# Layer 0's 32 experts as 24 tiles of 128 hidden units, earlier loads of their combine rows, and 64-row masks in layer 1's attention

## What the kernel computes

```python
scores = sigmoid(x @ gate_w.T)
topk_ids = top_k(scores + e_bias, 4)
combine = zeros(T, E) with the normalised scores at topk_ids
g = einsum('th,ehi->tei', x, w1)
u = einsum('th,ehi->tei', x, w3)
a = silu(g) * u * combine[:, :, None]
out = einsum('tei,eih->th', a, w2)
```

## Time and profile before

| | us |
|---|---|
| median of the three timed runs | 1730.03 |
| lowest and highest of them | 1722.28, 1730.83 |
| the profiled execution | 1734.56 |
| its span, first to last instruction | 1732.8 |
| PE, DVE, ACT, POOL busy | 1441.4, 1129.3, 692.5, 170.4 |
| mean granted TensorE clock | 0.884 of full |

### The profile page before, as it was taken

One profiled execution on the slowest core, in us unless ns is written; L12 is line 12 of the kernel. 1 busy time (PEld: TensorE's weight loads), 2 busy tenths in 40 slices (PEclk: granted clock), 3 DMA queues, 4 the chain that ended last, 5 costly groups with the idle time before them and its releaser, 6 DMA issues. The chain is left out here.

```text
span 1732.8 us, 20831 instructions
## 1 busy us (share of the span) xinstructions
PE 1441.4 (83%) x6716; PEld 852.5 (49%) x6716; DVE 1129.3 (65%) x1721; ACT 692.5 (40%) x1256; POOL 170.4 (10%) x205
## 2 busy tenths in 40 slices
PE   3889999999999999429999996731699999748996
PEld 3345555554545554226666664531344444225785
DVE  4645646464646552368999998573767776146997
ACT  1133333323232333025555553421156665524663
POOL 0000100001010100001111110021011211101110
PEclk9689999999999999759999997865589998767998
DMA  2000110101010101104444441005112220112220
GB/s 72 5 9 6 25 28 7 33 0 33 0 33 0 33 4 25 28 13 105 108 108 108 108 110 38 1 1 159 36 27 57 67 57 17 30 27 84 95 91 25
DMA packets 41517, 78.47 MB, mean 45 GB/s; under 512 B 18880, under 2 KB 31048, under 8 KB 36808
## 3 DMA queue, kind: packets, MB, share of 16 engines
q1 hardware_dynamic: 40304, 69.03, 15.1%
q0 software_dynamic: 1152, 8.65, 2.4%
HBM read 69.20 MB, written 7.93 MB: 45 GB/s over the span
## 5 line engine op out<-in xcount | busy, mean ns | idle before, releaser
L582 ACT ACTIVATE shared<-ps 128x1024 f32<-128x1024 f32 (+7 forms) x256 | 165.8, 650 | 408.5 <-PE ps L428 252.1
L1216 PE MATMUL ps<-qA 128*96 128x512 f32 (+1 forms) x1152 | 305.1, 401 | 13.1 <-DVE qA L1328 10.4
L444 PE MATMUL ps<-shared,Vg 128*65 128x512 f32 (+3 forms) x768 | 295.5, 494 | 7.5 <-ACT shared L582 4.3
L495 DVE TENSOR_REDUCE mraw<-ps 128x1 f32<-128x512 f32 (+3 forms) x304 | 196.9, 660 | 112.0 <-PE ps L395 83.7
L1216 PEld LDWEIGHTS ps<-qA 128*96 128x96 f32 (+1 forms) x1152 | 192.3, 172 | 98.4 <-DVE shared L1341 21.1
L900 DVE TENSOR_REDUCE mraw<-ps 128x2 f32<-128x1024 f32 (+3 forms) x160 | 175.0, 1116 | 92.2 <-PE ps L820 68.8
L944 ACT ACTIVATE shared<-ps 128x512 f32<-128x512 f32 (+2 forms) x320 | 154.5, 562 | 138.6 <-PE ps L836 138.4
L391 PE MATMUL ps<-kH,qA 128*128 128x512 f32 (+3 forms) x384 | 185.2, 512 | 17.0 <-DVE mraw L495 13.2
L426 PE MATMUL ps<-qA,kH 128*128 128x512 f32 (+3 forms) x384 | 191.0, 498 | 2.7 <-DMA qB<-mT 2.7
L1270 ACT CAST qA<-shared 96x512 fp32r<-96x512 f32 (+1 forms) x192 | 119.2, 621 | 163.1 <-DVE shared L1348 162.5
L1227 PE MATMUL ps<-qA,kH 96*128 96x512 f32 (+1 forms) x576 | 165.4, 396 | 4.0 <-DVE qA L1322 4.0
(11 more groups left out here) (254 smaller groups left out, 1695.0 us busy)
## 6 DMA issues: line engine op xcount, KB each, us to landing
shared<-comb SPq DMA_DIRECT2D x32, 768.0 KB, 5.1
rB<-a0rec_dram POOLq DMA_DIRECT2D x8, 1024.0 KB, 7.0
shared<-comb SPq DMA_DIRECT2D x8, 1024.0 KB, 4.5
q_split<-qA SPq DMA_DIRECT2D x8, 512.0 KB
qA<-q_split SPq DMA_DIRECT2D x16, 256.0 KB, 4.4
rB<-a1rec_dram SPq DMA_DIRECT2D x32, 128.0 KB, 2.7
e0wUp<-in_w SPq DMA_DIRECT2D x64, 48.0 KB, 4.4
wqk<-in_wqk SPq DMA_DIRECT2D x8, 192.0 KB, 2.4
```

The lines of the kernel that those rows point to most:

```text
L444: ins = nc.tensor.matmul(O[0:65, lo:hi], k.Vg[par][:, kt, :], k.PT[:, slot % PTR, lo:hi], start=(kt == 0), stop=(kt == 4 * ch + 3))
L495: ins = nc.vector.tensor_reduce(out, bank[:, 0:n_h * width].rearrange("p (h w) -> p h w", w=width), AX, ALU.max)
L582: nc.scalar.activation(k.PT[:, slot % PTR, kt * P:S], score_banks(slot)[:, kt * P:S], ACT.Exp, scale=scale).then_inc(p_full, 1)
L1216: ins = nc.tensor.matmul(bank[0:M, :], w[par][:, at:at + M], h[:, cols], start=(r == 0), stop=(r == 2))
```

## The change

Three edits:

1. The 32 x 96 hidden units of layer 0, 3072 in all, are laid out on the host as 24 tiles of 128, and `stage_experts` is called with E = 24, M = 128. A tile takes units of up to two experts. 32 units never straddle an expert, so a tile has four parts of 32 partitions, each with a combine row of its own. `comb0` becomes 96 x 2048: each expert's row is stored three times, by three transfers, and each tile's rows come by four transfers, each of which broadcasts one row to 32 partitions.
2. In `stage_experts`, SP's wait ahead of the combine rows is on `f_full` (DVE's L1348 of the expert before last is done) and no longer on `a_free` (PE's down projections of it are done). This holds for both layers.
3. In layer 1's attention, each mask matmul with 128 rows becomes two with 64 rows, the identity's and the mask's upper and lower half, and `i` = 0 reads them on partitions 0 to 63, `i` = 1 on partitions 64 to 127. For that a new constant `halves` of 128 x 512 is loaded first of all and cast to bf16.

```diff
 stage_load
+        halves = k.rB[:, 0:4 * P].rearrange("p (a n) -> p a n", a=4)
         first = [
-            (cT[:, :, :], a["cT"]), (wmod[:, 0, :], a["wmod"][:, 0, :]), (k.ident[:, :], a["ident"]),
+            (halves[:, :, :], a["halves"]), (cT[:, :, :], a["cT"]), (wmod[:, 0, :], a["wmod"][:, 0, :]), (k.ident[:, :], a["ident"]),
...
                 link(nc.vector.memset(k.one_col[:, :], 1.0))
+                link(nc.vector.tensor_copy(k.halves[:, :, :, :].rearrange("p a b n -> p (a b) n"), halves[:, :, :]))
 stage_attention8, max_job
                     if diagonal:
                         for slot in range(len(js)):
-                            for i in range(2):
-                                ins = nc.tensor.matmul(pair[:, i, (slot + 1) * w - P:(slot + 1) * w], k.ident_bf[:, :],
-                                                       k.masks[:, 1, :], start=False, stop=True,
-                                                       skip_group_check=True)
+                            for part in range(2):
+                                for i in range(2):
+                                    rows = row_tile(i, 64)
+                                    ins = nc.tensor.matmul(pair[:, i, (slot + 1) * w - P:(slot + 1) * w],
+                                                           k.halves[rows, 0, part, :], k.halves[rows, 1, part, :],
+                                                           start=False, stop=(part == 1), skip_group_check=True)
 stage_combine
                 sp.wait_ge(copied, NC)
-                sp.dma_start(comb_dram, k.cT[0:E, :]).then_inc(stored, 16)
-                sp.wait_ge(stored, 16)
+                rows = comb_dram.rearrange("(e r) t -> e r t", r=copies)
+                for r in range(copies):
+                    sp.dma_start(rows[:, r, :], k.cT[0:E, :]).then_inc(stored, 16)
+                sp.wait_ge(stored, 16 * copies)
 stage_experts
-        NLD = 16 * (1 + (bias is not None))
+        parts = comb_dram.shape[0] // E
+        NLD = 16 * (parts + (bias is not None))
...
                 def load(e, par):
-                    sp.dma_start(k.cb[0:M, par, :], comb_dram[bass.ds(e, 1), :].broadcast_to((M, T)))\
-                        .then_inc(ld[par], 16)
+                    for q in range(parts):
+                        sp.dma_start(k.cb[q * M // parts:(q + 1) * M // parts, par, :],
+                                     comb_dram[bass.ds(parts * e + q, 1), :].broadcast_to((M // parts, T)))\
+                            .then_inc(ld[par], 16)
...
-                        sp.wait_ge(a_free, JOBS * (2 * j + par - 1) + 2)
+                        sp.wait_ge(f_full, JOBS * (2 * j + par - 1))
                         load(2 * j + par, par)
 program
-        stage_experts(nc, k, "e0", 32, 96, 1, k.hT, a["w1"], a["w3"], a["w2"], None, comb0, None, finish0)
+        stage_experts(nc, k, "e0", 24, P, 1, k.hT, a["w1"], a["w3"], a["w2"], None, comb0, None, finish0)
```

More of the change, by code:

```diff
@@ L1053, in stage_combine @@
         comb = sb("comb", [P, NT, E])
+        copies = comb_dram.shape[0] // E
         pick = sb("pick", [P, NT, E])
@@ L1689, in program @@
         k.masks = sb("masks", [P, 2, P], BF16)
+        k.halves = sb("halves", [P, 2, 2, P], BF16)
         k.mod = sb("mod", [P, 2, 6, B])
@@ L1718, in program @@
         dram = lambda n, s: nc.dram_tensor(n, s, F32, kind="Internal").ap()
-        comb0, comb1 = dram("comb0", (32, T)), dram("comb1", (8, T))
+        comb0, comb1 = dram("comb0", (96, T)), dram("comb1", (8, T))
         q_dram, k_dram = dram("q_split", (NH, 32, T)), dram("k_split", (NKV, 32, T))
@@ L1823, in constants @@
     pos = np.arange(S, dtype=f)
+    halves = np.zeros((P, 2, 2, P), f)
+    for part in range(2):
+        rows = slice(part * 64, (part + 1) * 64)
+        halves[:, 0, part, :] = np.tile(np.eye(P, dtype=f)[rows], (2, 1))
+        halves[:, 1, part, :] = np.tile(masks[rows, 1, :], (2, 1))
     dec = np.exp(-pos / f(S)).astype(f).reshape(TPB, P).T
@@ L1829, in constants @@
     return {
-        "ident": np.eye(P, dtype=f), "masks": masks, "dec": dec, "rope": rope,
+        "ident": np.eye(P, dtype=f), "masks": masks, "halves": halves.reshape(P, 4, P), "dec": dec, "rope": rope,
         "iota": np.tile(np.arange(32, dtype=f), (P, 1)),
@@ L1834, in constants, with packed @@
     }
+def packed(w):
+    return w.transpose(1, 0, 2).reshape(D, 24, P).transpose(1, 0, 2)
 def layout(inp):
@@ L1867, in layout @@
         "wqk0": wqk, "wo0": wo0,
-        "w1": g["L0_ffn_w1"], "w3": g["L0_ffn_w3"], "w2": g["L0_ffn_w2"],
+        "w1": packed(g["L0_ffn_w1"]), "w3": packed(g["L0_ffn_w3"]), "w2": g["L0_ffn_w2"].reshape(24, P, D),
         "W1a": W1[:, :, 0:256], "W1b": W1[:, :, 256:512],
```

## The result

The median of four runs is 1659.58 us (1651.65 to 1663.41); that of before, in four runs, is 1728.3 us (1722.28 to 1730.83). The ratio is 0.9601, with a 95% interval of 0.9556 to 0.9646: some 69 us. The profiled execution took 1658.08 us, where that of before took 1734.56; the forecast was 1664.

A forecast was written before the change was run, and what follows sets the result against it. Layer 0's experts were taken as bound by DVE's instruction chain plus GpSimd's interference. Tiles -64.3, store +2.4, first rows +0.5, constant +1.2 and masks -7 made -67.2 us, forecast 1664; 1650 to 1680 held 8 in 10.

The forecast's parts named there:

- What bounds `e0`: Layer 0's experts: DVE's chain plus GpSimd's interference sets the beat; 24 tiles at 8.75 us replace 32 experts, -64.3 us.
- PE holds the beat: Rival, layer 0's experts: the longer block vanishes in PE's backlog, 4.2 us better, 1660; chance 0.05.
- The rows' landing: Layer 0's combine rows: four pieces land after 6.3 to 6.8 us, inside 8.7 thanks to the earlier wait; cost nothing.
- rows late: Rival: combine pieces land later than 8.7 us after the wait, DVE stands each tile; 1671 to 1688; chance 0.10.
- The store and the head: Before layer 0's experts: two more stores cost +2.4 us; the first tile's rows, wanted 7.2 us after issue, +0.5.
- The constant: First stage: loading 256 KB ahead of the awaited loads costs +1.2 us; DVE's cast of it costs 0.
- The masks: Layer 1's attention: 64-row masks avoid 0.15 us per group, at most 14 us of PE, half on the path: -7 us.
- halves cost more: Rival, layer 1's attention: half masks cost more than they save, +8 in place of -7, 1679 us; chance 0.08.
- each added load costs as much as a full one: Layer 1's attention masks: 256 more weight loads each cost as much as full ones; part of the 1679 us rival, chance 0.08.
- The sum: Whole kernel: -64.3 + 2.4 + 0.5 + 1.2 - 7 = -67.2 us, forecast 1664 us.
- Its side sums: Whole kernel: forecast's own range 1650 (all the masks' gain, no longer block) to 1676, and the times given to rivals.
- slower: Rival, layer 0's experts: combine pieces don't overlap and set the beat, about 1726, or 1764 at 3.0 us each; chance 0.02.

The follow-up runs named there:

- tiles_only: Changed kernel with the masks as before and without the new constant (edits 1 and 2 alone): 1666.8 us, ratio to before 0.9627.
- no_block: Changed kernel with GpSimd's subtraction cut to 8 columns of each low part: 1646.65 us in its one run.
- split_late: Changed kernel with ACT's copies of the next tile's weights moved behind the job's SiLU instead of ahead of it: 1645.51 us, ratio to before 0.9499.
- old_wait: Changed kernel with SP's wait ahead of the combine rows back on the down projections: 1696.29 us, ratio to before 0.9787.
- masks_only: Kernel before with edit 3 alone (new constant and 64-row masks): 1729.34 us, ratio to before 0.9983.
- full_twice: Changed kernel with each half mask as a 128-row matmul, zeros in the other half's rows, same matmul count: 1677.9 us, ratio to before 0.9696.

## Why the prediction was right, step by step

- **What bounds `e0`.** Right. The beat was DVE's chain plus GpSimd's block, per instruction and not per partition. `tiles_only` and the changed kernel give 8.72 and 8.71 us per tile (8.75 forecast), the landmarks -65.2 us (-64.3 forecast), L1316 takes 0.84 us, and the long L1358 1.23 (1.26 forecast). The growth is where it was looked for: the mean of the combine product over `e0` rose from 0.842 to 0.876 us, 0.14 per tile, which is the whole step from 8.57 to 8.71 (0.175 forecast). `no_block` shows the cause: without GpSimd's work the beat falls.
- **PE holds the beat (rival).** Wrong at 8.71, since `split_late` runs the same matmuls in 8.15. But PE was nearer than the step read as: the next bound lay 0.56 us below, not at DVE's 7.92.
- **The rows' landing.** Right that they fit, and tested: 6.9 us after the first issue, just above 6.3 to 6.8, with 1.6 us to spare (1.9 forecast). The picture of pieces that follow each other at 1.22 us is what the landings show (1.2). The transfers fill 0.64 x 8.76 = 5.6 us per tile (5.7 forecast). The statement that the cover is the earlier wait stands by `old_wait`: DVE then waits in 22 of the 24 tiles and 36 us of `e0` are lost. The rival *rows late* didn't come about, but it was one wait away.
- **The store and the head.** The sizes were 2.4 and 0.5, together 2.9, and the landmark shows +2.8. They are distributed otherwise. From the store's issue to the next stage's first weights it is +2.9 (5.9 us in every run with three stores), and the head of `e0` costs nothing (-0.1). So the total is partly luck: the store's term was 0.5 too small and the head's 0.6 too large.
- **The constant.** +1.2 forecast. The first sigmoid came at 11.05, 11.16 and 11.41 us in the three kernels without it, and at 11.68 to 12.83, 12.3 on average, in the nine that load it first: +1.1. The +1.6 of the two profiles above and the +1.0 of `masks_only` (12.07) lie within that scatter. The cast is hidden, as forecast: it runs at 13.81 us, and DVE still waits for PE 4.60 us behind it.

```profile
12.66 0.21 ACT L98 ACTIVATE cT_sig<-cT 128x4 f32<-128x4 f32 x1 [10.55 <-DMA wv<-in_wv]
...
13.81 0.43 DVE L123 CAST halves<-rB 128x512 bf16<-128x512 f32 x1
...
18.84 0.25 DVE L127 COPY mod<-ps 128x12 f32<-128x12 f32 x2 [4.60 <-PE ps L105]
```

- **The masks.** -7 forecast, about -6 at an equal clock, by the step that was named: between the two row shapes PE loses time ahead of the masks and behind them, and with masks in the shape of the scores less of it. What shows it is the same stage at an equal clock with as many passes in both shapes, and the medians of the groups: 0.54 to 0.39 us in the 64 smaller ones and 0.54 to 0.33 in the 32 larger. That is some 16 us of PE (14 forecast), so a bit over a third of it was on the path and not half. `full_twice` agrees, but its 15 us hold the cost of twice the passes too; they show that the rival *halves cost more* would have held for 128-row halves. Whether PE empties its array in the step isn't shown, only the time. ACT's wait on L840 fell from 138.4 to 124.6 us, more than the forecast 7, but part of that goes with the clock: `masks_only` has 131.6. The Trainium skill, "TensorEngine Tiling (Array Packing)", section "Key Properties", says that a change of mode drains the engine; the 0.33 us ahead of `full_twice`'s masks, and 0.24 without a change, agree with it. The rival that each added load costs as much as a full one did not come about: four loads and matmuls of 64 rows took the 0.29 us of two full ones.
- **The sum.** -67.2 forecast; the medians moved by about 69. The profiled executions moved by 76.6, and the 9.4 more than forecast is almost entirely the 8.8 that go with the clock in `a1`. That one execution has more time at 2.4 GHz than another isn't explained here; no run sets it. So the sum came out by its large term, which is shown to 1 us; the small ones are each near the limit of what these runs can tell.
- **Its side sums.** The lower end of the range is 1664 - 7 - 4.2 = 1653 and not 1650, and the *slower* rival's 1726 and 1764 start from the profiled execution, where the other rivals start from 1664. Neither changes the forecast.

## What to carry to other kernels

When the beat is a chain of instructions of fixed length, fill their partitions; but price what grows with the width, and look for the next bound at once (here PE, 0.56 us below). When a load is cut into transfers to few partitions, the room between its issue and its first use decides, and a wait that is worth nothing alone can be worth nearly half of the change with it. Before a profile's difference in a stage is put down to an edit, run the edit alone and hold the stage against others with the same clock.

## What the runs showed of the hardware

- GpSimd's subtraction holds up a DVE product with both operands in SBUF for most of the time that they overlap (1.23 us instead of 0.68 where 0.68 overlap, 0.85 instead of 0.69 where 0.30 do), and not a product that reads one operand from PSUM (0.69). Moving it from the one to the other took two moved `if`s and saved 13 us in `e0`.
- The same attention code took from 269.9 to 281.9 us, in step with the time that the granted clock stood at 1.2 GHz (54 to 88 us), 0.33 us for each. That is twice what the masks' new shape saved in it. Whether a lower clock makes the stage longer, or a stage that runs more loosely gets the lower clock, isn't told apart by these runs; `full_twice` took 284.85 us with 52.6 us at 1.2 GHz, so a long stage alone doesn't bring the lower clock.
- Four bf16 matmuls of 64 rows took 0.29 us, as did two of 128 rows, loads included; but with 64-row score matmuls around them the group took 0.34 us from pair to pair in the one shape and 0.66 in the other, for four masks each, in the groups shown (medians 0.39 and 0.65).
- Four broadcasts to 32 partitions each (256 KB a piece) landed 1.2 us apart though issued 0.52 apart, the last 6.9 us after the first issue; one to 128 partitions (1 MB) took 4.7 us.
- One store that repeats each source row three times brought the next stage on no sooner (6.4 us) than three stores (5.9 us).
